# Softplus of blocks 4 to 7 moved from the gap into the slots of the scan stage, in a Mamba, quantized MLP and mixture-of-experts layer

## What is computed

```python
# 1. state-space mixer, per batch: DI = 1024 channels, 16 states, 512 time steps
xz = einsum('ed,bld->bel', in_proj_weight, layernorm(x))    # x half and z half
x_ = silu(depthwise_conv(x half))
dt, Bc, Cc = split(x_proj_weight @ x_)
delta = softplus(dt_proj_weight @ dt + dt_proj_bias)
h_t = h_{t-1} * exp(delta_t * A) + (delta_t * u_t) * B_t     # scan over time
y_t = sum_n h_t[n] * C_t[n] + u_t * D
x = x + out_proj_weight @ (y * silu(z))
# 2. MLP with int8-like smooth quantization of inputs and weights (two linears)
x = x + quant_linear(silu(gate) * up),  gate, up = quant_linear(layernorm(x))
# 3. 16 experts, the two best of each token, and a shared expert of width 512
x = x + moe(layernorm(x)) + sigmoid(x @ shared_gate) * shared(x)
```

## Time and profile before

| what | us |
|---|---|
| runs | 1700.11, 1702.56, 1709.99; median 1702.56 |
| the profiled execution | 1698.6 (span 1696.8) |
| busy in the span: PE, DVE, POOL, ACT | 1445.6, 1349.2, 1065.7, 798.0 |
| first scan of stages 1, 2, 3 | 443.23, 826.19, 1208.23 |
| last scan of stage 1 | 699.24 |

### The profile page before, as it was taken

The page is one execution under the profiler, slowest core; times in us unless marked ns, Lnnn a source line. Parts: engine busy times, 40 slices in busy tenths (PEclk is TensorE's granted clock), DMA queues, the critical chain, the costliest instruction groups (busy, mean ns, idle before and its releaser), DMA issues.

```text
span 1696.8 us, 19403 instructions
## 1 busy us (share of the span) xinstructions
PE 1445.6 (85%) x5408; PEld 830.0 (49%) x5416; DVE 1349.2 (80%) x2215; ACT 798.0 (47%) x1368; POOL 1065.7 (63%) x684
## 2 busy tenths in 40 slices
PE   7867678999699899999699899999699999836994
PEld 3323223444465565444465565444465665325783
DVE  3488999676899999796899999796899999784212
ACT  3575454245734565245734565245734565222141
POOL 0299999101999899500999899500999999422101
PEclk9988899999699999999699999999699999967997
DMA  3550000412535674513535674512534774600984
GB/s 111 207 204 25 0 0 1 161 38 76 220 121 182 198 242 150 204 44 101 217 124 174 205 238 154 204 44 101 217 125 147 236 233 130 248 25 8 353 333 143
DMA packets 94074, 252.14 MB, mean 149 GB/s; under 512 B 11024, under 2 KB 11152, under 8 KB 88848
## 3 DMA queue, kind: packets, MB, share of 16 engines
q1 hardware_dynamic: 86688, 229.93, 39.9%
q0 software_dynamic: 5120, 16.78, 3.0%
q10 hardware_dynamic: 2160, 4.19, 0.6%
HBM read 207.87 MB, written 42.99 MB: 148 GB/s over the span
## 4 chain that ended last, share of the span: by engine, by line
PE 52%; DVE 18%; issue 13%; POOL 7%; ACT 7%; DMA 2%; DVEq 0%; POOLq 0%; SPq 0%; ACTq 0%
PE bank L1902 10%; PE bank L1780 6%; DVE bank L1253 6%; PE bank L2028 5%; PE bank L1795 4%; PE bank L1834 4%; PE bank L1839 4%; POOL work L659 4%; PE bank L1931 3%; PE bank L1828 3%; PE bank L1923 2%; PE bank L1803 2%; DVE work L1265 2%; PE bank L1802 2%; DVE pairs L1265 2%
## 5 line engine op out<-in xcount | busy, mean ns | idle before, releaser
L659 POOL TENSOR_TENSOR work<-du,BB 128x1024 f32<-128x1024 f32 x255 | 603.0, 2378 | 5.2 <-DVE work L1529 4.4
L926 ACT ACTIVATE bank<-delta,A_sb 128x512 f32<-128x512 f32 x512 | 349.9, 690 | 477.3 <-DVE pairs L1265 260.8
L1253 DVE TENSOR_TENSOR_SCAN bank<-bank,work 128x512 f32<-128x512 f32 x432 | 522.5, 1219 | 12.9 <-ACT bank L926 9.2
L1902 PEld LDWEIGHTS bank<-x3T,ew_up 128*128 128x128 f32 x1488 | 221.1, 196 | 74.5 <-issue 63.2
L1902 PE MATMUL bank<-x3T,ew_up 128*128 128x128 f32 (+1 forms) x1488 | 243.3, 310 | 5.2 <-issue 5.2
L1265 DVE TENSOR_TENSOR pairs<-bank,CB 128x512 f32<-128x512 f32 x240 | 160.9, 671 | 1.6 <-PE bank L1839 0.6
L604 POOL TENSOR_TENSOR col<-col,halfpow 128x4 f32<-128x4 f32 (+1 forms) x8 | 7.8, 973 | 209.8 <-DVE col L1405 209.8
L1265 DVE TENSOR_TENSOR work<-bank,CB 128x512 f32<-128x512 f32 x192 | 128.3, 668 | 0.0
L1795 PE MATMUL bank<-xT,wst 128*128 128x512 f32 x256 | 117.7, 604 | 8.4 <-ACT delta L873 6.6
L1834 PE MATMUL bank<-pairs,ident 128*128 128x512 f32 x160 | 90.6, 650 | 34.4 <-DVE zg L1273 18.8
L2028 PE MATMUL bank<-wst,zg 128*128 128x512 f32 x256 | 117.0, 593 | 0.9 <-DVE zg L1273 0.9
(11 more groups left out here) (243 smaller groups left out, 2518.2 us busy)
## 6 DMA issues: line engine op xcount, KB each, us to landing
ew_up<-in_exp_w SPq DMA_DIRECT2D x93, 512.0 KB, 3.8
ew_dn<-in_exp_w SPq DMA_DIRECT2D x93, 256.0 KB, 4.3
hm<-xs_dram SPq DMA_DIRECT2D x69, 256.0 KB, 4.6
ys_dram<-x3T SPq DMA_DIRECT2D x69, 256.0 KB, 4.5
wst<-in_w_in SPq DMA_DIRECT2D x64, 256.0 KB, 2.7
BB<-bc_dram SPq DMA_DIRECT2D x16, 1024.0 KB, 7.2
CB<-bc_dram SPq DMA_DIRECT2D x16, 1024.0 KB, 9.1
wst<-in_out_w SPq DMA_DIRECT2D x32, 256.0 KB, 2.9
```

What stands on the lines that cost most here:

```text
L659: nc.gpsimd.tensor_tensor(dBu[:, k % CHUNK_SLOTS, :, :], du[:, j % 2:j % 2 + 1, :].broadcast_to([P, 2, T]), BB[:, n0:n0 + 2, :], ALU.mult) ...
L926: nc.scalar.activation(R[q % RING][:, :], delta[:, j, :], ACT.Exp, scale=A_sb[:, j, n:n + 1]).then_inc(S["da_ready"], 1)
L1253: V.tensor_tensor_scan(prod[c % (2 * PAIR_SLOTS)] if on_pool(q) else R[q % RING][:, :], R[q % RING][:, :], dBu[:, c // 2 % CHUNK_SLOTS, c ...
L1902: ins = mm(gu_bank(v)[:, part * n:(part + 1) * n], w[:, part * D + k * P:part * D + (k + 1) * P], rhs, start=(k == 0), stop=(k == KD - 1))
```

## The change

- Delta of blocks 4 to 7 is written raw in the gap (`raw`: matmul plus bias, one copy on ACT). The rest of their softplus moves into the scan stage, by new tables `LATE_..._AT`: blocks 4 and 5 from slot 6 on, 6 and 7 from slot 32 on, two at a time in the four planes of `xT`. `one_more` of these blocks moves from DVE to ACT, the logarithm overwrites w and so waits for `lost`.
- POOL's differences of blocks 1 to 3 move from the gap to pair slots 2 to 4, its second chunk moves from the stage into the gap, ahead of the norm.
- The second row norm's apply moves to slots 1 and 2 of ACT, the copies of the router's inputs to slot 3.
- In the gap's second half PE does the transposes of the gated rows before z3 (it was behind it), all eight dl before z5, and z6 directly before the second quantized linear (it stood ahead of the weight scales; z7 is still behind the linear); ACT does the decays of the first three units before z7.
- A diagonal of its own for the skip (`skip_d`), and some small buffers laid over others.

The diff, cut to its core:

```diff
+LATE_ABS_AT = {4: 6, 5: 6, 6: 32, 7: 32}
+LATE_EXP_AT = {4: 7, 5: 7, 6: 33, 7: 33}
+LATE_RELU_AT = {4: 8, 5: 8, 6: 34, 7: 34}
+LATE_MORE_AT = {4: 9, 5: 9, 6: 35, 7: 35}
+LATE_LOST_AT = {4: 11, 5: 12, 6: 37, 7: 38}
+LATE_LN_AT = {4: 14, 5: 14, 6: 40, 7: 40}
+LATE_SUM_AT = {4: 8, 5: 9, 6: 21, 7: 22}
+LATE_INVERSE_AT = {4: 20, 5: 21, 6: 46, 7: 47}
+LATE_ERROR_AT = {4: 22, 5: 23, 6: 48, 7: 49}
+LATE_LESS_AT = {1: 2, 2: 3, 3: 4, 4: 13, 5: 14, 6: 26, 7: 27}
+ROW_NORM_AT = 1
+X3_AT = 3
...
@@ POOL, phase1
                     for i in range(4):
                         softplus_sum(a, i)
-                    for i in range(4):
-                        softplus_lost(a, i)
+                    softplus_lost(a, 0)
                     softplus_less(a, 0)
                     du_block(a, 0)
                     chunk(a, 0)
                     for i in range(1, 4):
-                        softplus_less(a, i)
+                        softplus_lost(a, i)
+                    chunk(a, 1)
                 if m is not None:
                     norm(2 * m + 1)
-                if a is not None:
-                    for i in range(4, 8):
-                        softplus_sum(a, i)
...
@@ POOL, scan_stage
-                        if k == 1 and b > 0:
-                            for i in range(4, 8):
-                                softplus_less(b, i)
+                        if b > 0:
+                            for i in range(1, NBLK):
+                                if LATE_LESS_AT[i] == k:
+                                    softplus_less(b, i)
+                                if i >= 4 and LATE_SUM_AT[i] == k:
+                                    softplus_sum(b, i)
...
@@ ACT
+            def raw(a, m):
+
+                sc.wait_ge(S["dl_ps"], NBLK * a + m + 1)
+                nc.scalar.activation(delta[:, m, :], dl_bank(a, m)[:, :], ACT.Identity, bias=dtb[:, m:m + 1]
+                                     ).then_inc(S["raw_ready"], 1)
...
@@ DVE, between
                 q1.maxima(0)
+                for i in range(4):
+                    one_more(a, i)
                 q1.scale(1)
                 q1.maxima(1)
                 q1.weight_diag()
                 for i in range(4):
-                    one_more(a, i)
+                    lost(a, i)
                 q1.integers(0)
-                for i in range(4):
-                    lost(a, i)
                 q1.integers(1)
...
                 row_stats(m, 2 * m + 1)
-                for i in range(4, 8):
-                    one_more(a, i)
-                for i in range(4, 8):
-                    lost(a, i)
```

More of the change, by code:

```diff
@@ L987, in y_rows @@
                     nc.scalar.copy(ys[n % 2], down_ps[1][:, :]).then_inc(S["y_ready"], 1)
-                if experts:
-                    for i in range(KD if scan else KD // 2):
+                if not scan:
+                    for i in range(KD // 2):
                         x3(i)
@@ L1039, in magic_rows, with row_norm @@
                                          bias=magic[:, 0:1]).then_inc(S["mg_ready"], 1)
-            def row_norm(m, l):
+            def row_norm(m, l, half=None):
                 src, dst = ((xn, x1n), (x2, xn))[l % 2]
                 sc.wait_ge(S["row_shifted"], l + 1)
-                for t in range(TT):
+                for t in range(TT) if half is None else (2 * half, 2 * half + 1):
                     nc.scalar.activation(dst[:, t, :], src[:, t, :], ACT.Identity, scale=rstd[:, t:t + 1],
@@ L1324, in scan_stage @@
                         scan_unit(p)
-                    if scan and p == 1 and b > 0:
-                        for i in range(4, 8):
-                            softplus(b, i)
+                    if scan and b > 0:
+                        for i in range(4, NBLK):
+                            if p == LATE_LOST_AT[i]:
+                                lost(b, i)
+                            if p == LATE_ERROR_AT[i]:
+                                softplus(b, i)
                     if scan and b == 0:
@@ L1703, in places @@
                     linkG(V.tensor_scalar(tiles, up, MAGIC, None, ALU.subtract))
-                    linkG(V.tensor_tensor_scan(sums, ones_row[:], tiles, 0.0, ALU.mult, ALU.add))
+                    linkG(V.tensor_tensor_scan(sums, ones[:, 0:NE], tiles, 0.0, ALU.mult, ALU.add))
                     linkG.mark(V.tensor_copy(first_tile[:, 1:NE + 1], sums))
```

175 lines of the change are left out of this document (106 added, 69 removed).

## The result

The changed kernel took **1768.87 us** (median of four runs, 1768.17 to 1772.79) where the kernel before took 1704.07 beside it (1700.11 to 1709.99): a ratio of 1.038, with a 95% interval of 1.035 to 1.042. The forecast was 1731, the range 1705 to 1749. It is slower, as forecast, and by more than twice as much: 70.9 us between the two profiled spans, where 28.8 had been worked out. Of the 42.1 us in excess, 32.0 lie in the three stages with their gaps, and 10.1 outside them, where nothing had been forecast.

What follows compares the result with a forecast made beforehand. No engine was taken as always busy; POOL's order in slots 16 to 32 was the tightest place. Per stage 6.1 + 3.5 = 9.6 us, three 28.8, on 1698.6: 1727.4, plus 4.0 for the median: 1731 us, range 1705 to 1749.

Steps and rivals of the forecast that it cites:

- Handover: From one scan stage to the next: slot 5 at 453.9 us instead of 463.15, 9.2 us earlier.
- POOL's order up to unit 32: Block 4's sum at pair slot 8 waits 11 us for the logarithm; chunk 9 at 484.4, unit 32 6.1 us later.
- Slots 33 to 60: Rest of the stage: operations 3.6, logarithms 0.6, wait for POOL perhaps 0.5, about 1.2 hidden: +3.5 us.
- the medians of stage 0: Durations of lost and error operations beside scans, 0.90 and 1.065 us, less 0.08 overlap each: 1.8 us a block.
- POOL's lead comes back: From slot 33 on POOL gets ahead again (by 3 us until unit 42 in the trace); DVE and PE set the pace.
- Rival 3: Behind slot 33, DVE's four two-SBUF-operand operations each wait a whole POOL chunk (2.34 us): +9 us a stage, 1758; chance 0.11.
- Stage 0: The first scan stage: no change in its time was forecast; the sum counted only three stages of 9.6 us.
- the lower bound: DVE keeps 9.2 us until slot 14, unit 32 3.1 late, later costs lowest: a stage 5.5 us late, 1719.
- ScalarE's tables: In the slots, four table loads of 1.28 us a stage, a switch costing 1.3 without drain; with drain, 1735.

Runs made afterwards that it cites:

- the later sums: The changed kernel with POOL's sums of blocks 4 to 7 moved from pair slots 8, 9, 21, 22 to 10, 11, 24, 25: 1736.85 us.
- the pairs: DVE's lost and error operations put two to a slot: 1713.80 us against the kernel with the later sums, 1763.87 us against the changed kernel.
- errors on POOL: The kernel with the later sums, with the four error products of blocks 4 to 7 on POOL instead of DVE, subtractions two pair slots later: 1741.26 us.

## Why the prediction was right and where it failed

- **Handover: right.** Forecast 9.2 us earlier at slot 5. The logits' maximum came at 458.66, less stage 0's 5.7: 10.2 earlier than 463.15. The wait in front of it was forecast as some 6 us and was 8.09; unit 4 had been 18 us early. POOL's norm was forecast as the late thing. It was late (443.10), but the runs showed that making it earlier is not enough, with the row norm behind the decays.

```profile
458.66 0.23 DVE L1718 TENSOR_REDUCE hm<-bank 128x4 f32<-128x64 f32 x1 [8.09 <-PE bank L1903]
```

- **POOL's order up to unit 32: right.** Forecast: the sum of block 4 waits for the ln some 11 us, chunk 9 at 484.4, unit 32 6.1 later. Measured: 12.98 us of wait, chunk 9 at 490.10 less 5.7, which is 484.4, and unit 32 +6.1. That this wait costs is shown by the later sums with the pairs in both kernels (10.7 us at unit 32), less by the later sums alone (1.3 there).

```profile
486.33 1.27 POOL L639 TENSOR_TENSOR delta<-delta,xT 128x512 f32<-128x512 f32 x1 [12.98 <-ACT xT L929]
...
490.10 2.36 POOL L673 TENSOR_TENSOR work<-du,BB 128x1024 f32<-128x1024 f32 x1
```

- **Slots 33 to 60: the step that failed.** I wrote +3.5 us, with 3.6 for four operations "by the medians of stage 0", 0.6 for the ln and 0.5 for POOL's wait. Measured: +15.0 (from +6.1 to +21.1). Lost of block 6 cost 6.2, the second wait of POOL some 2.6, the errors of blocks 6 and 7 4.1, and a wait for PE in slot 54 3.0, where TensorE ran at the 1.2 GHz level from 579.4 to 586.2, after 1.68 us of work in the 5 us from 575 to 580; 0.9 of that came back behind unit 64. The working took a median for something that has no typical value. Stage 0's list held the outlier (2.521) beside the median 0.900; my own text said that POOL's lead would be used up at unit 32, five slots ahead of the lost operation of block 6.
- **"POOL's lead comes back"** was right as a fact and wrong as a comfort: in the changed kernel POOL ran three more operations while one DVE operation stood still (540.76).
- **Rival 3 was the mechanism**, at 0.11. Its price (each operation held up by one chunk, 2.34 us, +9 for a stage behind slot 33, 1758) was near the truth but shaped wrongly: one of 6.42 and three short ones (0.67, 1.53, 2.73), not four equal ones. That 1758 lies near 1768.87 is in part luck: 10.1 us of the measured time lie outside the stages, and the PE wait wasn't in it. The Trainium skill ("SBUF — State Buffer", Who interferes with whom) says that a DVE instruction with two SBUF inputs contends with a GpSimd instruction that reads SBUF. The trace agrees (27.4 us for an operand moved from PSUM to SBUF). The same section has the later one wait until the first finishes; some waits were that (the errors of blocks 6 and 7), others spanned two to five POOL operations, so here the measurement decides.
- **Stage 0** was taken as unchanged. Its 5.7 us come from the same hold-up falling the other way, in instructions that the change doesn't touch; the difference of the two kernels doesn't show it. The 4.4 us behind the last scan I didn't follow further; in the other kernels that piece was -0.6 to 6.1.
- **Slips that moved little:** 15.8 less 2.1 plus 0.6 is 14.3 and not 14.4, and the lower bound was worked out as 1719 and then written as 1717.
- **ScalarE's tables: right.** The load in slot 14 took 1.28 us and its ln began 1.30 behind it; nothing of a drain.

```profile
484.33 1.28 ACT L929 ACT_TABLE_LOAD   x1
485.63 1.15 ACT L929 ACTIVATE xT<-xT 128x512 f32<-128x512 f32 x2
```

## What to carry to other kernels

Before work goes from an idle gap into a stage where VectorE and GpSimd both run full, look at where its operands lie: an operation with two SBUF operands can cost there what GpSimd still has to do before it pauses, however small it is, so keep one operand in PSUM, or try such operations directly behind each other. Read the lead of one engine over the other at the very slot, in a kernel that has the other waits of the change in it. And an operation put into a slot of an in-order engine inherits the wait of whatever opens that slot.

## What the runs showed of the hardware

- A DVE operation with two operands in SBUF was often held up over two to five back-to-back POOL operations that read SBUF, the one that was running included. It then ended 0.54 to 0.56 us behind the end of POOL's last one for 512 elements a partition (547.18 and 546.63; 516.37 and 515.81; 522.65 and 522.09; 545.05 and 544.51), and 0.02 behind it for one element (191.90 and 191.88). The longest: 8.56 us for 512 elements (errors on POOL, batch 3), 8.43 for 4, 7.33 for 1.
- The 432 products that read PSUM and SBUF had a mean of 0.67 us in both kernels, beside a busy POOL, and none above 0.9.
- A pause of 0.17 us of POOL, ahead of an indirect DMA, was enough to end a hold-up.
- In other cases DVE got in behind the POOL operation that was running, with no pause in POOL's work, and POOL's next operation took some 0.45 us longer (1.72 instead of 1.27 behind the errors of blocks 6 and 7; two chunks 5.57 instead of 4.65 in stage 0 of the kernel before, DVE's operation 1.20). Both outcomes were seen for the same instructions in stage 0, with the same distance between the engines; what decides stays open.
- The profile counts a held-up operation as busy: DVE was "97% busy" from 540 to 560 while it held the stage up.
